# Linear attention over eight steps: the next step's values in a tile of their own, turnings and projections in earlier slots, and features multiplied over 128 rows

## The reference, cut to what matters

```
q, k, v = split(x @ Wqkv + bqkv)                 # 16 heads of 16
features(y): yn = y / max(norm(y), 1e-12)        # per head
             arg = clip((yn @ omega[r, h]) * sqrt(2 s_r) - s_r, -20, 20)
             f = exp(arg) / sqrt(32) * sqrt(w_r) # r = 0, 1; 32 each: 64 per head
qf, kf = features(q), features(k)
# causal, in chunks of 128 rows (8 steps), with a running state:
out = (state_kv . qf + sum over j <= i of (qf_i . kf_j) v_j) / max(the same with 1 for v, 1e-6)
y = layernorm(x + out @ Wout + bout)
```

## Time and profile before

| | us |
|---|---|
| median of 3 runs | 1460.28 (1456.12 to 1461.38) |
| the profiled execution | 1456.94 |
| its span, first to last instruction | 1455.3 |
| TensorE busy, products | 1351.5 (93%) |
| VectorE / ScalarE / GpSimd busy | 926.7 / 684.9 / 547.3 |
| attention stage | about 321 to 777 |

### The profile page before, as it was taken

One profiled execution on the slowest core, in us unless ns is written; L12 is line 12 of the kernel. 1 busy time (PEld: TensorE's weight loads), 2 busy tenths in 40 slices (PEclk: granted clock), 3 DMA queues, 4 the chain that ended last, 5 costly groups with the idle time before them and its releaser, 6 DMA issues. The chain is left out here.

```text
span 1455.3 us, 33730 instructions
## 1 busy us (share of the span) xinstructions
PE 1351.5 (93%) x12000; PEld 1186.4 (82%) x12000; DVE 926.7 (64%) x1947; ACT 684.9 (47%) x1258; POOL 547.3 (38%) x500
## 2 busy tenths in 40 slices
PE   6989999987989899888898999999999999999995
PEld 5778888875767677767676988888899999999984
DVE  4757767677777877877875464444555555555547
ACT  2356676543544544554454433222355555555533
POOL 0144555451345454354311007422344444444421
PEclk7699999999999999999999999999999999999998
DMA  6343343115546636647345404633688888888885
GB/s 226 123 146 111 111 147 112 67 37 128 129 121 172 178 120 180 162 127 187 102 128 201 181 30 157 265 105 122 177 230 232 233 234 235 234 236 234 250 260 204
DMA packets 113086, 241.29 MB, mean 166 GB/s; under 512 B 21617, under 2 KB 77297, under 8 KB 105841
## 3 DMA queue, kind: packets, MB, share of 16 engines
q1 hardware_dynamic: 88768, 185.05, 41.9%
q0 software_dynamic: 23088, 54.31, 13.2%
q10 hardware_dynamic: 1152, 0.93, 0.2%
HBM read 150.23 MB, written 64.84 MB: 148 GB/s over the span
## 5 line engine op out<-in xcount | busy, mean ns | idle before, releaser
L2696 PE MATMUL ps<-e_xhl,s_whl 128*128 128x256 f32 x1848 | 245.7, 282 | 0.2 <-DVE e_g L2775 0.2
L2696 PEld LDWEIGHTS ps<-e_xhl,s_whl 128*128 128x128 f32 x1848 | 231.0, 189 | 0.4 <-issue 0.4
L2078 PE MATMUL ps<-s_xhl,s_whl 128*128 128x512 f32 x660 | 164.1, 397 | 1.4 <-PEq L1094 1.4
L2527 POOL DMA_INDIRECT xs<-e_y,e_slot_id x78 | 122.3, 1568 | 92.6 <-ACT e_y L2561 73.7
L499 POOL TENSOR_TENSOR b_hhl<-b_h,b_hhl 128x512 fp32r<-128x512 f32 x64 | 94.2, 1475 | 140.3 <-ACT b_hhl L750 119.8
L2078 PEld LDWEIGHTS ps<-s_xhl,s_whl 128*128 128x128 f32 x660 | 121.8, 190 | 26.4 <-issue 1.8
L2675 PE MATMUL ps<-s_whl,e_ghl 128*128 128x256 f32 x936 | 139.4, 285 | 0.5 <-issue 0.5
L2775 DVE TENSOR_TENSOR e_g<-ps,e_act_h 128x256 f32<-128x256 f32 x156 | 66.2, 424 | 112.4 <-ACT e_act_h L2574 111.2
L2675 PEld LDWEIGHTS ps<-s_whl,e_ghl 128*128 128x128 f32 x936 | 122.0, 189 | 0.9 <-issue 0.7
L594 PE MATMUL ps<-b_w,b_hhl 128*128 128x256 f32 x768 | 105.4, 287 | 7.6 <-DVE b_turned_rows L854 5.4
L1560 ACT ACTIVATE c_qf<-c_cf,fc 128x512 f32<-128x512 f32 x64 | 46.3, 723 | 137.3 <-DVE c_cf L1695 137.3
(11 more groups left out here) (382 smaller groups left out, 2719.3 us busy)
## 6 DMA issues: line engine op xcount, KB each, us to landing
s_whl<-wlo SPq DMA_DIRECT2D x38, 1024.0 KB, 5.1
s_fs<-s_stage SPq DMA_DIRECT2D x192, 128.0 KB, 2.6
s_whl<-wlo SPq DMA_DIRECT2D x38, 512.0 KB, 3.7
c_eraw<-in_expert_w POOLq DMA_DIRECT2D x24, 512.0 KB, 5.1
wlo<-c_elo POOLq DMA_DIRECT2D x24, 512.0 KB, 3.1
wall<-in_expert_w SPq DMA_DIRECT2D x8, 1536.0 KB, 10.0
xg<-b_zeros POOLq DMA_DIRECT2D x13, 780.0 KB, 4.0
e_xr<-xg SPq DMA_DIRECT2D x39, 260.0 KB, 3.8
```

The costliest lines, as they stand in the source:

```text
L2078: mm = pe.matmul(ps[:, H + 2 * (m % 2) + w, :], whl[:, wp, e, lo:lo + P], xhl[:, k, xp, kd, :], start=q == 0, stop=q == 3 * KD - 1)
L2527: gp.indirect_dma_start(xs, bass.IndirectOffsetOnAxis(ap=slot_id[:, i, b:b + 1], axis=0), y[:, k, b, :], None, compute_op=ALU.add).then_in ...
L2696: mm = pe.matmul(ps[:, H + m, w * SLOT:(w + 1) * SLOT], whl[:, k, wp, lo:lo + P], xhl[:, k, xp, kd, :], start=q == 0, stop=q == 3 * KD - 1)
```

## The change

Values of step i+1 are projected at slot 5 of step i and written to a new tile `vnext`, and ScalarE copies them to `va` in slot 1 (`next_values`). For space `kf` shrinks from four buffers to two. The tables are rewritten: FT goes from slot 2 to 0, FQ from 2 and 3 to 1 and 2, FN all to slots 6 and 7, BO, BC and BW around them. The norm chain's VectorE parts move from slots 3, 4 and 5 to 3 and 4, the row moments from slot 1 to 0. In the first body, FV of step 0 is called FU, all four FM stand at its start. On GpSimd the residual add moves behind the squares and two expert chunks change places; SP loads the residual right after the copies of the second half step. `features` multiplies 128 rows, and GpSimd clears rows 96 to 127 of both `fs` tiles, and `va`, once at the start.

```diff
-        kf = sb("kf", [P, 4, TOK])
+        kf = sb("kf", [P, 2, TOK])
+        vnext = sb("vnext", [P, BATCH, D])
...
-        SLOTS_OF_X = {0: ((A_, "FN", 1), (B_, "FN", 3), (C_, "BO", 2)),
-                      1: ((A_, "BC", 0), (C_, "FV", 0), (C_, "FV", 1)),
-                      2: ((A_, "FT", 0), (A_, "FT", 1), (B_, "BO", 3), (C_, "FQ", 0), (C_, "FQ", 1)),
-                      3: ((A_, "FQ", 2), (B_, "FQ", 3), (C_, "BC", 1)),
+        SLOTS_OF_X = {0: ((A_, "FT", 0), (A_, "FT", 1), (C_, "BO", 2)),
+                      1: ((A_, "FQ", 0), (B_, "FQ", 1), (C_, "BC", 0)),
+                      2: ((A_, "FQ", 2), (B_, "FQ", 3)),
+                      3: ((A_, "BO", 3),),
                       4: (),
-                      5: ((C_, "BW", 0),),
-                      6: ((B_, "FN", 0), (B_, "FN", 2), (C_, "BW", 1)),
-                      7: ((A_, "BO", 0), (C_, "BO", 1))}
+                      5: ((A_, "FV", 0), (A_, "FV", 1), (B_, "BO", 0), (C_, "BC", 1)),
+                      6: ((A_, "FN", 0), (A_, "FN", 2), (B_, "BO", 1), (C_, "BW", 0)),
+                      7: ((A_, "FN", 1), (A_, "FN", 3), (C_, "BW", 1))}
-        FIRST_OF_X = {0: ((Z_, "FV", 0), (Z_, "FV", 1), (Z_, "FT", 0), (Z_, "FT", 1), (Z_, "FM", 0), (Z_, "FM", 1), (Z_, "FQ", 0),
-                          (A_, "FN", 1), (B_, "FN", 3), (C_, "FQ", 1)),
+        FIRST_OF_X = {0: ((Z_, "FU", 0), (Z_, "FM", 0), (Z_, "FM", 2), (Z_, "FU", 1), (Z_, "FT", 0), (Z_, "FT", 1),
+                          (Z_, "FM", 1), (Z_, "FM", 3), (Z_, "FQ", 0), (A_, "FQ", 1)),
                       1: ((A_, "FQ", 2), (B_, "FQ", 3)),
...
+                      5: ((A_, "FV", 0), (A_, "FV", 1), (B_, "BO", 0)),
+                      6: ((A_, "FN", 0), (A_, "FN", 2), (B_, "BO", 1)),
+                      7: ((A_, "FN", 1), (A_, "FN", 3))}
+        LAST_OF_X = {0: ((C_, "BO", 2),), 1: ((A_, "BC", 0),), 2: ((C_, "BO", 3),), 3: ((C_, "BC", 1),),
+                     4: ((C_, "BW", 0),), 5: ((A_, "BW", 1),), 6: (), 7: ()}
...
@@ sync @@
-                k1 = (i, "FN", 3) if half else (0, "FM", 1) if isinstance(i, int) and i == 0 else (i - 1, "FN", 2)
+                k1 = (0, "FM", 2 + half) if isinstance(i, int) and i == 0 else (i - 1, "FN", 2 + half)
...
                 if is_step(i):
                     stack(i, 1)
+                if is_step(i - 2):
+                    sp.wait_ge(s["x_free"], x_index(i - 1, "BW", 1) + 1)
+                    sp.dma_start(xb[:], x2[i - 1]).then_inc(s["res_in"], 16)
...
-        EXPERT_AT = (0, 1, 2, 5)
+        EXPERT_AT = (0, 2, 4, 6)
@@ gpsimd @@
-                if is_step(i - 1):
-                    gp.wait_ge(s["res_in"], 16 * i)
-                    gp.tensor_tensor(xb[:], xb[:], bo[:].unsqueeze(1).to_broadcast([P, BATCH, D]), ALU.add).then_inc(s["xb_ready"], 1)
                 if not isinstance(i, int) or 1 <= i < LAST:
                     split_expert_weights(i, range(1))
                 if is_step(i - 2):
                     row_roots(i - 1)
-                if not isinstance(i, int) or 1 <= i < LAST:
-                    split_expert_weights(i, range(1, 2))
                 if is_step(i + 1):
...
                         gp.tensor_tensor(sq[:, bb], qk[:, bb], qk[:, bb], ALU.mult).then_inc(s["sq_ready"], 1)
+                if is_step(i - 1):
+                    gp.wait_ge(s["res_in"], 16 * i)
+                    gp.tensor_tensor(xb[:], xb[:], bo[:].unsqueeze(1).to_broadcast([P, BATCH, D]), ALU.add).then_inc(s["xb_ready"], 1)
                 if not isinstance(i, int) or 1 <= i < LAST:
-                    split_expert_weights(i, range(2, EPER - 1))
+                    split_expert_weights(i, range(1, 2))
                 if is_step(i + 1):
                     gp.wait_ge(s["rnorm_ready"], f)
...
-                    split_expert_weights(i, range(EPER - 1, EPER))
+                    split_expert_weights(i, range(2, EPER))
...
+            for half in range(2):
+                gp.memset(fs[half][STACK:P].bitcast(F32), 0.0).then_inc(s["fs_cleared"], 1)
+                gp.wait_ge(s["fs_cleared"], half + 1)
+            gp.memset(va[:], 0.0).then_inc(s["va_cleared"], 1)
+            gp.wait_ge(s["va_cleared"], 1)
+            gp.memset(va[:, :, :, HD:HD + 1], 1.0).then_inc(s["va_cleared"], 1)
@@ tensor @@
+                if isinstance(i, int) and i == 0:
+                    pe.wait_ge(s["fs_cleared"], t // QUAD + 1)
                 for q in range(2):
-                    pe.matmul(ps[:, FB + q, :], om[0:STACK, t, :], fs[t // QUAD][0:STACK, t % QUAD, q, :],
+                    pe.matmul(ps[:, FB + q, :], om[:, t, :], fs[t // QUAD][:, t % QUAD, q, :],
...
                 if u == 0:
-                    pe.wait_ge(s["x_free"], x_index(i, "FV", 1) + 1)
+                    pe.wait_ge(s["va_ready"], i + 1)
@@ scalar @@
                 wait(act, "pair_done", n - 3)
+                wait(act, "kt_done", n - 1)
...
+            def next_values(i):
+                if isinstance(i, int) and i == 0:
+                    act.wait_ge(s["va_cleared"], 2)
+                    act.wait_ge(s["x_free"], x_index(0, "FU", 1) + 1)
+                else:
+                    act.wait_ge(s["x_free"], x_index(i - 1, "FV", 1) + 1)
+                    act.wait_ge(s["pair_done"], PAIRS * i)
+                act.activation(va[:, :, :, 0:HD], vnext[:].rearrange("p b (h d) -> p b h d", h=HEADS1), ACT.Copy).then_inc(s["va_ready"], 1)
...
                     x_high(i, t, C_)
+                    if t == 1 and is_step(i):
+                        next_values(i)
...
-                    if t in (3, 4) and is_step(i - 2) and not last_rows(i):
+                    if t in (2, 3) and is_step(i - 2) and not last_rows(i):
@@ vector @@
-                            wait(ve, "pair_done", PAIRS * step)
...
+                        elif name in ("FU", "FV"):
+                            if a == 0:
+                                wait(ve, "va_ready", step)
+                            ins = ve.tensor_tensor(vnext[:, 2 * a:2 * a + 2, :], src.rearrange("p (b n) -> p b n", b=2),
+                                                   bq[:, 2 * D:].unsqueeze(1).to_broadcast([P, 2, D]), ALU.add)
@@ vector, body(i) @@
                     if pair(i, t, 1) is not None:
                         mask(*pair(i, t, 1))
-                    if is_step(i - 2) and not last_rows(i) and t == 1:
+                    if is_step(i - 2) and not last_rows(i) and t == 0:
                         rows.turn(i - 2)
                         rows.n = BATCH
                         row_moments(rows)
-                    if front and t == 4:
-                        squares(norm, i + 1, 1)
-                        norm_guess(norm)
-                    if front and t == 5:
-                        norm_newton(norm, False)
-                        norm_newton(norm, True)
-                        norm.end()
-                    x_evac(i, t, B_)
-                    if pair(i, t, 2) is not None:
-                        new_state(*pair(i, t, 2))
                     if is_step(i - 2) and not last_rows(i) and t == 1:
                         row_guess(rows)
-                    x_evac(i, t, C_)
                     if front and t == 3:
                         squares(norm, i + 1, 0)
                     if front and t == 4:
                         norm_newton(norm, False)
+                    x_evac(i, t, B_)
+                    if pair(i, t, 2) is not None:
+                        new_state(*pair(i, t, 2))
+                    x_evac(i, t, C_)
+                    if front and t == 3:
+                        squares(norm, i + 1, 1)
+                        norm_guess(norm)
+                    if front and t == 4:
+                        norm_newton(norm, False)
+                        norm_newton(norm, True)
+                        norm.end()
...
-            ve.memset(va[:], 0.0).then_inc(s["cleared"], 1)
             ve.memset(state[:], 0.0).then_inc(s["cleared"], 1)
-            ve.wait_ge(s["cleared"], 1)
-            ve.memset(va[:, :, :, HD:HD + 1], 1.0).then_inc(s["cleared"], 1)
```

More of the change, by code:

```diff
@@ L1174, in x_list @@
         def x_list(i):
-            slots = FIRST_OF_X if isinstance(i, int) and i == 0 else SLOTS_OF_X
+            slots = FIRST_OF_X if isinstance(i, int) and i == 0 else LAST_OF_X if last_rows(i) else SLOTS_OF_X
             return [(t, point, name, a) for t in range(PAIRS) for point, name, a in slots[t] if is_step(step_of(i, name, a))]
@@ L1185, in x_before @@
             return count(2) * i + (x_before(1, kinds) - count(1))
[L1187 removed]
+        ALL = ("FT", "FQ", "FU", "FV", "FN", "FM", "BO", "BC", "BW")
         def x_events(i):
@@ L1266, in body @@
                     stack(i + 1, 0)
-                if is_step(i - 1) and (not isinstance(i, int) or i < STEPS):
-                    sp.wait_ge(s["x_free"], x_index(i, "BW", 1) + 1)
-                    sp.dma_start(xb[:], x2[i]).then_inc(s["res_in"], 16)
                 if isinstance(i, int) and i == LAST:
```

(20 more changed lines are left out.)

33 lines of the change are left out of this document (11 added, 22 removed).

## The result

The kernel after takes 1418.3 us (median of 4 runs, 1416.4 to 1419.4), the kernel before 1458.2 on the same chip (4 runs, 1452.3 to 1461.4). The profiled execution took 1419.4 us (span 1417.8), 37.5 less than that of before.

A forecast was written before the change was run, and what follows sets the result against it. TensorE sets the pace, with only its pauses and half clock to save. Six steps -15, start and step 0 -5.4, step 7 -3.5 make about -24 us: 1433 profiled, 1437 as median, range 1425 to 1453.

The forecast's parts named there:

- Slots 3 to 5: VectorE falls behind TensorE there; features 0 to 0.3 us late, BO0 0.9 late, pause 1.0 to 1.5 a step.
- 1.0 for small waits that a walk doesn't find: Allowance of 1.0 us in each of the six steps between the ends, added to the walk's pauses.
- Moments in slots 0 and 1: Row moments may meet GpSimd's chunk 0 and delay FQ1; taken as 1.0 us a step, ends 0 and 2.4.
- 3 us of half clock left: In the six steps a third of the present half clock stays, added to 319.2 to give 322.
- rival B: No gain: a new wait as long as the old ones, or half clock every step; 1453 to 1464; chance 0.11.
- Step 0: First step: 37.7 us of work, about 5.3 of pauses and 3 of clock, 46 instead of 48.3.
- Turnings FN: Slots 6 and 7: the 1.7 us pause for GpSimd's normalising goes in each step, with over 3 us spare.
- the copy: ScalarE's copy of the values to `va` in slot 1, about 1.4 us, hidden with 2.5 over; the 7.7 us go.
- 128 rows: Features over 128 rows instead of 96: taken as 0, ends -3 to +3 us; no clock gain counted.
- The ends: First features near 331.4, start and step 0 together -5.4 us, step 7 -3.5, behind the stage 0.
- A: Pauses move: VectorE's jam in slots 3 and 4 isn't covered, moments caught each time; -15, 1445 us; chance 0.20.
- C: Slower: GpSimd's two long operations meet the norm chain of slots 3 and 4; +20, 1480 us; chance 0.07.

The follow-up runs named there:

- run 4: Kernel after with the row moments behind BO2's evacuation in slot 0, so that GpSimd's chunk 0 catches them; 1426.3 us, ratio 0.979.
- run 1: Kernel after with features over 96 rows again, all else kept; 1417.3 us, ratio 0.973.
- run 8: Kernel after with FV0 in slot 4, BO3 at the end of slot 2 and BC1 at the end of slot 3; 1413.4 us, ratio 0.969.
- run 9: Kernel after with ScalarE's copy into `va` made three times, the third releasing the context; 1423.7 us, ratio 0.977.
- run 6: Kernel after with the norm chain in its old places in slots 3, 4 and 5; 1427.8 us, ratio 0.979.
- run 5: Kernel after with GpSimd's chunk 2 ahead of the normalising, so that it meets the Newton turns; 1436.5 us, ratio 0.984.
- run 7: Kernel after with the values' projection over two slots, FV0 in slot 4 and FV1 in slot 5; 1408.7 us, ratio 0.967.
- run 10: Kernel after with FV0 in slot 4 and, in slot 6, BO1 ahead of the scores and FN0, FN2 behind them; 1414.2 us, ratio 0.970.
- run 3: Kernel before with only the row moments moved from slot 1 to slot 0; 1454.8 us, ratio 0.9985.

## Why the prediction was wrong, point by point

The direction and the mechanism (pauses go, and the clock comes back with them) were right, and the sum was a third short: -24 against -37.5 in the profiled execution. By its terms 13.9 are missing: 12.2 in steps 1 to 6 and 3.5 in step 0, while the start and the end gave 1.8 less than forecast. The 12.2 are the moments (6), the half clock (3), the allowance for small waits (2.9 of its 6) and 0.3 of slots 3 to 5: three terms were sized too large, and the largest was a collision entered at half price that didn't take place.

**Slots 3 to 5: right in sum.** The walk gave features 0 to 0.3 late and BO0 0.9 late, 1.0 to 1.5 in all. Measured 0.54 and 1.06, each a little over; over the six steps 8.7 us (2.6 and 6.1) where the sum took 9.

**"1.0 for small waits that a walk doesn't find": twice too large.** There is one such wait, 0.52 in slot 6 for the bank of BC1, 3.1 us in six steps against 6. The prediction gives no source for its 1.0. In the kernel before five kinds of small waits make 12.5 us, 2.1 a step, and none of the five is left after.

**Moments in slots 0 and 1, taken at 1.0 between 0 and 2.4: failed.** They miss chunk 0 by 0.3 us, in steps 2 to 6 none of their operations takes over 0.17 us in after, and TensorE waits for nothing in these slots. The bounds held (run 4: 1.3 a step when hit, behind BO2's evacuation), the choice didn't: an event that happens in every step or in none was entered as its middle, which is no possible outcome. It was two cases, and the one without a hit, 6 us less, came. It came by 0.3 us, less than the half microsecond to which the walk was good: that the change gained these 6 us is luck.

**"3 us of half clock left": failed.** None is left in steps 1 to 6. All 8.5 us of busy time came back. The sum kept a third of it, although the reason given against rival B said 0: the clock fell after 1.80 and 3.05 us, not after 1.46, and no pause as long as 1.8 was left in the walk. That reason gave the right result but was read from L1400's waits alone. In before the clock fell in step 4 a second time, behind a wait of 1.73 us for GpSimd, and in step 2 behind one of 2.01 for the copies into `fs`; behind the wait for GpSimd in step 2, of 1.70, it stayed whole:

```profile
481.78:487.78 6.00, 5.73 (x80) 4.75 (x82) 3.77 (x6) 3.18 (x6) 5.31 (x4) 1.00 0.19 40
...
594.15:600.15 6.00, 6.00 (x70) 4.77 (x71) 2.77 (x5) 3.18 (x6) 5.27 (x4) 0.72 0.19 40
```

The runs show for steps 1 to 6: longest pause 1.06 to 1.14 (after, runs 1, 4, 8, 9), clock 1.00 in all; 2.12 (run 6), it falls in every second one; 3.09 (run 5), in five of six.

**Step 0: mis-sized, 46 against 42.5.** Busy is 38.7 at 0.96 and 37.5 at 1.00 (run 7), as in the 37.7 of the sum; the clock costs 1.2 and not 3, the pauses 3.8 and not 5.3. The 37.7 came out, but doesn't follow from its own 7 of pauses and 6 of clock (48.3 - 13 + 4.1 = 39.4). What the earlier places of the norm chain are worth here run 6 shows: with the old ones the step takes 47.25, with a wait of 2.60 for GpSimd and the clock at 0.93.

**Turnings FN, the copy, the queues, 128 rows: right.** The 10.2 us for GpSimd and the 7.7 us for the values are gone; the copy takes 1.05 us (1.4 was given) with 3.3 of cover (2.5 was given), and in steps 1 to 6 it can be made three times (in step 7 even the one copy is waited for, for 0.4 us, and three cost 3.7: run 9); normalising stands 6 us idle for the root; 96 rows give the same time. That the 10.2 were the norm chain's is shown by run 6; that the 7.7 were the values' is read from who ends the wait, as no run puts them back into `va` alone.

**The ends: right to about 1 us each, with one term wrong.** First features at 332.7 (331.4 forecast). Step 7 gave more than forecast (-4.8 to its last features, -3.5 forecast), and "behind the stage: 0" failed: 1.8 are lost there, behind a wait at the stage's end that grew by 2.35 with the residual add at the end of GpSimd's queue. Over runs 1 and 4 to 10 the first features stand between 332.5 and 336.1. In after and in each of these runs the stretch from the stage's first product to them takes 11.6 to 11.9 us where its granted clock is 0.85 or 0.86, 12.2 and 12.3 at 0.79 and 0.78, and 13.9 at 0.68. The part from step 7 on takes 729.4 to 735.1. So a difference of 2 us ahead of the first features, or of 4 from step 7 on, says nothing of an edit that doesn't touch that part.

**The rivals.** A put the jam of slots 3 and 4 on the path; FV covers most of it, and run 7 shows what covering all brings, 1.3 us a step. C's mechanism is real: run 5 makes one hit of 2.3 a step and costs 18 us. In steps 1 to 6 of after it is absent, because no VectorE operation of a form that was held in any run meets a long one of GpSimd there. The chain's sums of squares do (from 501.79, chunk 1 runs from 501.03 to 503.44), and keep their 1.21 us; the guess starts at 504.36, 0.9 us behind the chunk. GPSIMD Engine Reference of the Trainium skill, section Key points, has GpSimd contend with VectorE instructions in a 2-port perf mode or with two SBUF inputs; run 5 agrees for the 128x128 Newton operation (2.33 us instead of 0.28), run 4 for the 128x4 addition (2.36 instead of 0.15).

**The range.** Its low end took only one of the 1.0 terms and the clock away, which is -24 - 6 - 3 = -33, or 1427; the 1425 that stands there is 2 lower than its own terms. With the moments missed, no small waits and no half clock, all three of which its text named as open, it would have been -24 - 6 - 6 - 3 = -39, or 1421. Even that is 3 above the measured time; step 0 makes up the 3.5.

## What to carry to other kernels

A walk of the new order, instruction by instruction against the engine that is behind, gave the pauses of slots 3 to 5 to half a microsecond; the allowance on top of it was twice what the walk had missed, so it needs a source like any other term. What happens in each step or in none (a collision, a fall of the clock) is a branch with its own total and not a half-priced term. And projections that need nothing from the lagging engine are best placed in the slots where it lags: two slots for them instead of one brought 7.6 us here in steps 1 to 6, on top of what the change gave. An operation moved in a loop body is also moved in the last round: what stands last on a queue there can set when the next stage starts.

## What the hardware showed that was not expected

The clock doesn't answer to a pause's length alone. In step 0 of after it falls behind a pause of 1.15 us (0.72 over the 6 us from 350.68), and in run 7 the same pause, 1.16 at 350.87, is followed by 1.00. In run 6 every step has the same 2.12 us wait, and the mean granted clock is 0.97 and 1.00 in turn; in run 5 every step has 3.1 us, and one is at 1.00, one at 0.94. A single VectorE operation a step that GpSimd holds is enough to bring falls about: 2.0 us of pause became 2.0 to 4.2 us a step (53.73 and 55.94 against 51.7).

The VectorE operations that GpSimd holds last until GpSimd's ends, whatever their own size: 128x4 for 2.36 us and 128x128 for 2.33, beside GpSimd operations of 2.36 and 2.35 that started with them, and 1.35 where GpSimd's had started 1.07 earlier (run 3). Held were small operations whose inputs and output all lie in SBUF. Not all of these are: the sums of squares (1.21) and the 128x16 reciprocal (0.25) kept their length beside the same GpSimd operations, and so did those with an input in PSUM (clip 1.33, state 0.28).

Products of 512 columns take 432 ns over 96 rows and over 128 (run 1), and neither form changes the clock.
